# Reordered first stage, one-operation normalisation and DMA-turned last projections in an attention and feed-forward kernel

## The chip, the cores and the metric

One core of one Trainium2 chip runs the whole program. The metric is the device time of one execution in microseconds (us), lower is better. Durations of single operations come from one profiled execution.

## What is computed

A transformer block on x of 4 x 1024 x 512: layer norm without scale, causal attention with 16 heads of width 32, and a gated feed-forward of width 1536 whose weights are rounded to fp8 values. Both branches read the normalised x, and both are added to x.

```python
xn = _layernorm(x, axis=-1)
q, k, v = xn @ Wq.T, xn @ Wk.T, xn @ Wv.T            # split into 16 heads
scores = einsum('bhqd,bhkd->bhqk', q, k) / sqrt(32)  # causal mask, softmax
attn = einsum('bhqk,bhkd->bhqd', probs, v) @ Wo.T
fuse = silu(xn @ gate_w8 * gate_scale) * (xn @ up_w8 * up_scale)
out = x + attn + (fuse @ down_w8) * down_scale
```

## The kernel before

TensorE works on fp16. A float32 operand is split into a high and a low fp16 part (HI, LO), and a product is the sum of three terms, HI x HI, HI x LO and LO x HI (`TERMS`). Each engine has its own program, written out by hand; tables of step numbers (`PROJ_STEP`, `GATE_STEP`, `HEADS_LOADED` and so on) say at which step an engine does what, and semaphores couple the engines. Nothing is scheduled by a planner. SP issues nearly all DMAs, in the order of its program; a wait in it holds up every DMA behind it.

**First stage** (`prepare`). x is taken in 8 tiles of 512 tokens. A tile is 12 chunks of 12 matmuls of 512 columns: four chunks for q, four for k, four for v (L904). ACT copies each chunk's high part out of PSUM (L575, L579), DVE subtracts for the low part (L796, L800), SP stores it. Beside that, for the next tile: DVE takes the statistics (L601, L605) and normalises (L615), POOL computes the reciprocal root in 14 small operations (L468 to L476) and the low part of x (L485), ACT the high part (L512, `x_high`), and SP turns both parts by DMA transposes (L382, `turn_x`). TensorE begins a tile when both parts are turned. Only tile 0 is turned on TensorE, and so are the weights (L842, `turn_weights`), which need a power-of-two scale: DVE takes a maximum (L634, `weights_max`), TensorE spreads it over the partitions (L867, `spread_max`), DVE reads it back (L652, `weights_power`). DVE also rounds the feed-forward weights in 24 parts (`magnitude`, `add_step_of`, `take_step_off`). A chain of small DVE operations (L747 to L760, `feed_forward_factors`) follows the last chunk, and then all engines meet at the end of the block.

**The loop** (`attend`). 16 iterations of 4 heads, each head in 9 steps, 36 steps k to an iteration. In every head TensorE computes transposed scores (L1426), row scores (L1440, L1444) and the row maxima of a later head (L206), and multiplies probabilities with values (L1464). ACT does the exponentials, ACT, POOL and DVE the splitting, and SP turns the last two rows of probabilities (L1073). `normalise` on DVE (L1302 to L1316) closes each half of a head:

```python
nc.vector.tensor_copy(o_low[:, :, :], o_half[:, :, 0:DK])
nc.vector.reciprocal(rsum[:, :], o_half[:, :, 2 * DK])
nc.vector.tensor_tensor(o_sum[:, :, :], o_half[:, :, DK:2 * DK], o_low[:, :, :], ALU.add)
nc.vector.tensor_tensor(dst, o_sum, rsum broadcast, ALU.mult)
```

The feed-forward of two blocks of 128 tokens is spread over an iteration (L1488, L1502). From iteration 4 on, the output projection of two blocks is added (L1519): ACT and POOL split them into `a_part` (steps 12 and 20), SP turns them (L1110), TensorE projects at steps 20 to 22 and 28 to 30, DVE adds the result (L1331), SP stores it. Each head's maxima reach TensorE through a small DMA (L196, `store_row`), which the next head's first scores wait for.

**The end.** The last iteration leaves eight blocks to project. TensorE first finishes the last head's values and two feed-forward blocks (L1502). DVE scales these (L1340), POOL adds them (L1143), and then POOL makes the low parts (L1147). TensorE turns each block by 8 transposes (L1512), DVE copies it out of PSUM (L1323), TensorE projects. There are two buffers.

Of the kernel before, what the change touches and what calls it, by code (L numbers as in the profile page):

```python
# [37 lines left out]
TERMS = ((HI, HI), (HI, LO), (LO, HI))  # L38
EPS = 1e-5
# [23 lines left out]
FF_LOADED = {(1, 0): ((0, 1), (1, 1)),  # L63
             **{(t, 6): ((2, t),) for t in range(1, NT - 1)},
             **{(t, 8): ((0, t + 1),) for t in range(1, NT - 1)},
             **{(t + 1, 0): ((1, t + 1),) for t in range(1, NT - 1)}, (NT - 1, 4): ((2, NT - 1),)}
X_LOADED = {**{(t, 4): t + 2 for t in range(1, NT - 2)}, (0, 7): 2}


HEADS_LOADED = {(2, 3): 0, (2, 6): 1, (3, 3): 2}  # L70
# [69 lines left out]
GATE_STEP = {4: 0, 6: 1, 8: 2, 14: 3, 16: 4, 18: 5, 19: 6, 23: 7, 25: 8, 27: 9, 31: 10, 33: 11}  # L140
# [128 lines left out]
def prepare(nc, x, weights, ffn, scales, xn_dram, keep, rows, bank):  # L269
# [11 lines left out]
    with ExitStack() as ctx:  # L281
# [6 lines left out]
        w_raw = [sb(f"w_raw{m}", [P, KC, D], F32) for m in range(3)]  # L288
# [85 lines left out]
        def _(sp):  # L374
            def turn_x(w, t):
# [14 lines left out]
            for m in range(3):  # L390
                load_weights(m)
            sp.wait_ge(w_hi_done, 1)
# [3 lines left out]
            def tile(t, par):  # L396
# [11 lines left out]
                for c in range(8):  # L408
# [9 lines left out]
                    if (t, c) == (NT - 1, 3):  # L418
                        store_row(sp, rows, 0, 1)
                    dst = (q_dram if c < 4 else k_dram).rearrange(  # L420
# [74 lines left out]
        def wmax_bank(m):  # L495

            return bank[(2, 2, 5, 0)[m]][:, 0:P]
# [6 lines left out]
        def _(act):  # L504
# [38 lines left out]
            def load_scales():  # L543
                gate_s, up_s, down_s = scales
                with nc.allow_non_contiguous_dma(reason="two vectors of 1536 scales"):
                    act.dma_start(gs[:, :], gate_s.rearrange("(c p) -> p c", p=P)).then_inc(small_loaded, 16)
                    act.dma_start(us[:, :], up_s.rearrange("(c p) -> p c", p=P)).then_inc(small_loaded, 16)
                act.dma_start(ds_row[:, :], down_s.rearrange("(a d) -> a d", a=1).broadcast_to([P, D])).then_inc(
                    small_loaded, 16)

# [14 lines left out]
            def tile(t, par):  # L565
                for c in range(12):
# [18 lines left out]
                    if (t, c) == (5, 2):  # L585
                        load_scales()
# [8 lines left out]
        def _(dve):  # L595
# [92 lines left out]
            weights_power(1)  # L688

# [72 lines left out]
            def factors_of_weights():  # L762
# [7 lines left out]
            first_tile = {0: ("max 2",), 1: ("power 2",), 2: ("statistics",), 3: ("low 2",), 4: ("normalise",),  # L770
                          6: ("magnitude 0",), 7: ("add 0",), 8: ("off 0", "magnitude 1"), 9: ("add 1",), 11: ("off 1",)}
            last_tile = {0: ("magnitude 20", "add 20"), 1: ("off 20",), 2: ("magnitude 21",), 3: ("add 21",),
                         4: ("off 21", "magnitude 22"), 5: ("add 22",), 6: ("off 22",), 7: ("magnitude 23", "add 23"),
                         8: ("off 23",), 9: ("maxima",), 11: ("factors",)}

            def plan_of(t):
                if t in (0, NT - 1):
                    return last_tile if t else first_tile
                a, b, c = (f"{3 * t - 1 + i}" for i in range(3))
                w3 = {(2, 11): ("max 3",), (3, 5): ("power 3",), (4, 11): ("low 3",)}  # L780
                return {0: ("statistics",), 1: ("magnitude " + a,), 2: ("normalise",), 3: ("add " + a,),
                        4: ("off " + a, "magnitude " + b), 5: ("add " + b,) + w3.get((t, 5), ()), 6: ("off " + b,),
                        7: ("magnitude " + c,), 8: ("add " + c,), 9: ("off " + c,),
                        11: w3.get((t, 11), ())}

            def tile(t, par):
                plan = plan_of(t)
                for c in range(12):
                    for m in WEIGHTS_COPIED.get((t, c), ()):
                        copy_weights(m)  # L790
                    if t == c == 0:
                        weights_low(1)
                    dve.wait_ge(hi_done, 12 * t + c + 1)
# [8 lines left out]
                    for what in plan.get(c, ()):  # L802
# [19 lines left out]
                        elif has_next(t):  # L822
                            {"statistics": norm_statistics, "normalise": normalise}[name](t + 1)
# [11 lines left out]
        def _(pe):  # L835
# [32 lines left out]

            pe.wait_ge(ident_set, 1)
# [4 lines left out]
            spread_max(1)  # L874

            def tile(t, par):
                for c in range(12):
                    if c == 0:

                        if t == 0:  # L880
                            pe.wait_ge(xt_act, 2)
                            pe.wait_ge(xt_dve, 2)
                        else:
                            for w in range(2):
                                pe.wait_ge(x_turned[w], 16 * t)
                    if t == 0 and c in (0, 3):

                        pe.wait_ge(wpow_set, 2 + c // 3)
# [7 lines left out]
                    for wp, xp in TERMS:  # L896
                        for kc in range(KC):
# [3 lines left out]
                            else:  # L901
# [3 lines left out]
                                                  stop=((wp, xp) == TERMS[-1] and kc == KC - 1))  # L905
# [6 lines left out]
                    if t >= NT - 2:  # L912
# [6 lines left out]
                        if head == 1 and c == 0:  # L919
                            turn_maxima(nc, pe, rows, bank[7], ident, 0)  # L920

            over_tiles(tile)

            pe.wait_ge(rows.m_red, 2 * NM)
            pe.wait_ge(ffspread, 1)
            nc.tensor.matmul(bank[0][:, :], ones[:, :], spread[:, :, :].rearrange("p n q -> p (n q)"), start=True,
                             stop=True).then_inc(ffmax_mm, 1)
# [3 lines left out]
def attend(nc, x, out, xn_dram, keep, rows, pair, bank):  # L931
# [5 lines left out]
    with ExitStack() as ctx:  # L937
# [22 lines left out]
        o_low = sb("o_low", [P, QB // 2, DK], F32)  # L960
# [3 lines left out]
        xt = sb("xt", [P, 2, KC, FT], F16)  # L964
# [6 lines left out]
        o_sb = [sb(f"o_sb{i}", [P, D], F32) for i in range(2)]  # L971
# [5 lines left out]
        o_sum = o_bank[:, 512 - QB // 2 * DK:512].rearrange("p (i d) -> p i d", d=DK)  # L977

        q_loaded, v_loaded, row_loaded, mt_copied = rows.q_loaded, rows.v_loaded, rows.row_loaded, rows.mt_copied
        xt_loaded = sem("xt_loaded")  # L980
# [32 lines left out]
        turn_mm = sem("turn_mm")  # L1013
        turned = sem("turned")
        late_turned = sem("late_turned")
# [22 lines left out]
        def row_width(r):  # L1038
# [5 lines left out]
        late_part = [probs[0][:, HI, i * 2 * D:(i + 1) * 2 * D].rearrange("p (w d) -> p w d", w=2)  # L1044
                     for i in range(2)]
        late_t = [probs[0][:, LO, i * 2 * D:(i + 1) * 2 * D].rearrange("p (w k t) -> p w k t", w=2, k=KC)
                  for i in range(2)]

        def late(i, r):

            return 2 * (r - (NIT - LAG)) + i
# [6 lines left out]
        def _(sp):  # L1058
# [7 lines left out]
            load_tile(0)  # L1066
# [9 lines left out]
            def iteration(it, with_out):  # L1076
                for s in range(HEADS_PER_IT):
# [19 lines left out]
                    if with_out and s in (1, 2):  # L1097
                        turn_attention(s - 1, it - LAG)
# [19 lines left out]
            for r in range(NIT - LAG, NIT):  # L1118
                for i in range(2):
# [572 lines left out]
```

## Time and profile before

| | us |
|---|---|
| three runs, median (lowest to highest) | 1330.88 (1330.05 to 1332.48) |
| profiled execution, its own time | 1335.85 |
| its span, first to last instruction | 1334.1 |
| tile 0 of the first stage | 0 to 69.19 |
| tiles 1 to 5 | 69.19 to 236.04 |
| tiles 6 and 7 | 236.04 to 304.55 |
| between the stages | 304.55 to 309.33 |
| loop and the last head | 309.33 to 1285.98 |
| the end | 1285.98 to 1334.1 |

Busy shares of the span: TensorE 94%, DVE 81%, ACT 67%, POOL 65%. The share is a mean over stages with different limits. A row of the timeline gives start, duration, engine, line and operation, and in brackets how long the engine sat idle before it and who ended that. A run of matmuls on one line is merged (x24); its end is modelled and reaches a little past the start of the next one.

### The profile page before, as it was taken

Reading aid. Unit: us, or ns where it says so; the run is one execution under the profiler, and the core shown is the slowest. Engines: PE = TensorE matmul, PEld = TensorE weight load, DVE = VectorE, ACT = ScalarE, POOL = GpSimd, SP = SyncE. Lnnn points to the kernel's source line nnn. Section 1 sums busy time; section 2 is a strip of 40 time slices with the busy share of each in tenths; the row PEclk is TensorE's granted clock in tenths of the full one; section 3 lists DMA queues with packets and bytes.
Section 4 is the critical chain, followed back from the end, with each engine's and each line's share of the span. In section 5 each row is a group of like instructions: output and inputs, shape, how many; then the busy total and the mean of one; then the engine's idle time right before and its main releaser. Section 6 shows DMA issues by size and latency. Waiting matters only on the chain.

```text
span 1334.1 us, 32685 instructions
## 1 busy us (share of the span) xinstructions
PE 1253.1 (94%) x11812; PEld 829.4 (62%) x11813; DVE 1076.6 (81%) x2752; ACT 895.9 (67%) x1527; POOL 871.5 (65%) x1016
## 2 busy tenths in 40 slices
PE   4999999997898999999999999999999999999987
PEld 2444444344776667676767676677767676676754
DVE  7777778777888888888888798988888888888753
ACT  3322223225878787788878787888878787888841
POOL 1322222204777777787888788878878888888753
PEclk8999999997999999999999999999999999999999
DMA  7489899664555554567656675756675666756441
GB/s 255 116 240 255 238 237 231 180 169 111 110 121 126 118 128 93 129 116 164 120 138 138 119 159 122 160 108 148 121 155 120 139 141 126 157 120 155 81 91 64
DMA packets 419152, 193.98 MB, mean 145 GB/s; under 512 B 330800, under 2 KB 388144, under 8 KB 418992
## 3 DMA queue, kind: packets, MB, share of 16 engines
q1 hardware_dynamic: 397328, 174.84, 57.9%
q10 hardware_dynamic: 21664, 17.05, 4.6%
q8 instruction: 94, 1.54, 0.5%
q14 instruction: 66, 0.54, 0.1%
HBM read 72.89 MB, written 42.21 MB: 86 GB/s over the span
## 4 chain that ended last, share of the span: by engine, by line
PE 33%; POOL 16%; ACT 8%; DVE 7%; issue 6%; DMA 4%; SPq 2%; ACTq 0%; DVEq 0%
PE bank L1488 12%; POOL row L1169 8%; PE bank L1502 8%; PE bank L1464 5%; DMA xt<-xn_parts 3%; POOL fuse L1151 3%; PE pair L206 3%; PE pair L1426 3%; ACT probs L1216 2%; SPq L1073 2%; ACT row L1240 2%; ACT fuse L1255 2%; POOL probs L1035 2%; PE pair L1519 2%; DVE row_top L1359 2%
## 5 line engine op out<-in xcount | busy, mean ns | idle before, releaser
L1226 ACT ACTIVATE p<-pair,s_exp 128x512 f32<-128x512 f32 (+1 forms) x384 | 243.3, 634 | 161.2 <-PE pair L1426 159.7
L1169 POOL TENSOR_TENSOR row<-row 128x896 f16<-128x896 f32 (+1 forms) x128 | 256.1, 2010 | 11.5 <-ACT row L1240 11.4
L1216 ACT CAST probs<-p 128x512 f16<-128x512 f32 (+1 forms) x384 | 214.7, 559 | 14.4 <-POOL p L1163 13.5
L1035 POOL TENSOR_TENSOR probs<-p,probs 128x512 f16<-128x512 f32 x192 | 221.2, 1156 | 0.2
L1488 PE MATMUL bank<-xt,wg 128*128 128x256 f16 x1536 | 204.1, 277 | 7.2 <-DMA xt<-xn_parts 4.7
L1488 PE MATMUL bank<-xt,wu 128*128 128x256 f16 x1536 | 204.0, 277 | 0.0
L1502 PE MATMUL bank<-wd,fuse 128*128 128x512 f16 x768 | 190.6, 378 | 0.9 <-DVE ff_out L1340 0.9
L1163 POOL TENSOR_SCALAR_AFFINE_SELECT p<-p 128x128 f32<-128x128 f32 (+1 forms) x256 | 108.5, 428 | 110.6 <-ACT p L1226 108.6
L1359 DVE TENSOR_REDUCE row_top<-pair 128x1 f32<-128x896 f32 (+1 forms) x128 | 147.2, 1150 | 24.0 <-PE pair L1444 24.0
L1488 PEld LDWEIGHTS bank<-xt,wg 128*128 128x128 f16 x1536 | 141.8, 99 | 36.8 <-DMA xt<-xn_parts 11.0
L1488 PEld LDWEIGHTS bank<-xt,wu 128*128 128x128 f16 x1536 | 144.3, 99 | 23.0 <-issue 0.2
L1151 POOL TENSOR_TENSOR fuse<-fu,fuse 128x512 f16<-128x512 f32 x96 | 113.9, 1186 | 63.1 <-ACT fuse L1255 62.8
L1233 ACT ACTIVATE row<-pair,row_bias,s_exp 128x896 f32<-128x896 f32 (+1 forms) x128 | 148.2, 1158 | 0.5 <-DVE row_bias L1362 0.3
L1426 PE MATMUL pair<-q_st,k_st 98*128 98x256 f16 (+3 forms) x640 | 137.4, 280 | 6.3 <-PEq L281 4.8
L229 DVE CUSTOM_DVE_ANT_0 junk<-pair,mask 128x128 bf16<-128x128 f32 x252 | 117.0, 483 | 29.9 <-PE pair L206 27.5
L1464 PE MATMUL bank<-v_sb,probs 128*128 128x65 f16 x2688 | 134.0, 192 | 2.8 <-DVE attn L1314 2.8
L206 PE MATMUL pair<-k_st,q_st 96*128 96x128 f16 x504 | 125.4, 309 | 11.1 <-issue 6.4
L1464 PEld LDWEIGHTS bank<-v_sb,probs 128*128 128x128 f16 x2688 | 119.6, 97 | 25.8 <-issue 3.2
L1240 ACT CAST row<-row 128x896 f16<-128x896 f32 (+1 forms) x128 | 126.7, 990 | 0.0
L1035 DVE TENSOR_TENSOR probs<-p,probs 128x512 f16<-128x512 f32 (+1 forms) x192 | 124.6, 662 | 2.3 <-ACT probs L1216 2.3
L1347 DVE SCALAR_TENSOR_TENSOR ga<-th,bank 128x256 f32<-128x256 f32 x192 | 79.7, 415 | 34.3 <-ACT th L1247 32.8
L1502 PEld LDWEIGHTS bank<-wd,fuse 128*128 128x128 f16 x768 | 68.3, 97 | 60.2 <-DVE ff_out L1340 1.4
(153 smaller groups left out, 2160.0 us busy)
## 6 DMA issues: line engine op xcount, KB each, us to landing
q_st<-q_parts SPq DMA_DIRECT2D x192, 64.0 KB, 2.6
k_st<-k_parts SPq DMA_DIRECT2D x192, 64.0 KB, 2.0
v_parts<-res SPq DMA_DIRECT2D x8, 1056.0 KB, 6.5
v_sb<-v_parts SPq DMA_DIRECT2D x64, 132.0 KB, 2.2
xn_parts<-x_t SPq DMA_DIRECT2D x16, 512.0 KB, 7.6
q_parts<-qk_st SPq DMA_DIRECT2D x32, 256.0 KB, 4.5
k_parts<-qk_st SPq DMA_DIRECT2D x32, 256.0 KB, 4.1
xt<-xn_parts SPq DMA_DIRECT2D x16, 512.0 KB, 4.6
```

The costliest lines, as they stand in the source:

```text
L206: nc.tensor.matmul(banks[u % len(banks)][:, 0:w], rows.q_st[i][part, blk * P:(blk + 1) * P], rows.k_st[i][part, k0:k0 + w], start=True, st ...
L1035: ops.tensor_tensor(probs[n % 2][:, LO, at], p32[e % RING][:, 0:UNIT_WIDTH[u]], probs[n % 2][:, HI, at], ALU.subtract).then_inc(signal, 1)
L1151: nc.gpsimd.tensor_tensor(fuse_pair(LO, p), fu[p % FU][:, :], fuse_pair(HI, p), ALU.subtract).then_inc(fuse_lo, 1)
L1169: nc.gpsimd.tensor_tensor(row16[r][:, w:2 * w], row32[r][:, :], row16[r][:, 0:w], ALU.subtract).then_inc(row_lo, 1)
L1216: nc.scalar.copy(probs[n % 2][:, HI, u * 512:u * 512 + w], p32[e % RING][:, 0:w]).then_inc(p_hi, 1)
L1226: nc.scalar.activation(p32[e % RING][:, 0:w], st_bank[u % 2][:, 0:w], ACT.Exp, scale=s_exp[:, :]).then_inc(exp_done, 1)
L1240: nc.scalar.copy(row16[r][:, 0:row_width(r)], row32[r][:, :]).then_inc(row_hi, 1)
L1359: nc.vector.tensor_reduce(row_top[:, r:r + 1], row_bank[r][:, 0:row_width(r)], AX.X, ALU.max).then_inc(row_red, 1)
L1426: mm = nc.tensor.matmul(st_bank[u % 2][:, at:at + w], k_st[s][:, j * P:(j + 1) * P], q_st[s][:, q0:q0 + w], start=True, stop=True)
L1464: mm = nc.tensor.matmul(o_half[:, i % (QB // 2), :], probabilities(n, i, j, part), v_sb[s][:, j, 0:VN], start=(j == 0 and part == HI), sto ...
L1488: mm = nc.tensor.matmul(ff_bank[f % 2][:, h * FT:(h + 1) * FT], (wg8, wu8)[h][:, kc, f * P:(f + 1) * P], xt[:, part, kc, :], start=(part = ...
L1502: mm = nc.tensor.matmul(misc[:, :], fuse[:, part, f, i * P:(i + 1) * P], wd8[:, f, :], start=(f == 0 and part == HI), stop=(f == FC - 1 an ...
```

## The change

- `X_TERMS`: in the first stage the term with the low part of x comes last, and `x_half_there` lets TensorE begin a tile when the high part is turned; the low part is waited for before the third group of four matmuls of chunk 0.
- Tile 0: the spreading of the second weight's maximum moves behind chunk 0, the third weight's maximum (`weights_max(2)`) ahead of the tiles, the third weight is turned after chunk 5 (before: 4) and evacuated at chunk 6 (before: 5); the second is turned after chunk 2 as before, and DVE evacuates it a chunk earlier.
- Each later tile: x is split (`x_high`) after chunk 2 (before: 4), the turns stand behind the stores of chunks 3 and 5 (before: 5 and 7), statistics are taken at chunk 10 of the tile before, normalisation at chunk 0. Feed-forward parts are loaded and rounded about one part earlier; the three early heads are loaded at the start of tiles 3, 4 and 5. The scales are loaded by SP at the beginning, not by ACT in tile 5.
- End of the first stage: the spreading of the feed-forward maxima goes behind chunk 8 of tile 7, and the factors are computed at chunk 9. The first `xt` is loaded in tile 7. `w_raw[0]`, `xt` and `o_sb` share one buffer.
- Loop: `normalise` sums both halves in one reduction. Gate 6 moves from step 19 to 22, the first projection from 20..22 to 19..21, its addition from 23 to 22. SP issues the turn of `a_part` ahead of the output store and `store_row`. A small memset moves from DVE to POOL.
- The end: four buffers; SP turns the eight blocks; TensorE and DVE do no turning. POOL makes the first four low parts ahead of the two additions; the values of row block 3 are computed ahead of the feed-forward products.

```diff
+X_TERMS = ((HI, HI), (LO, HI), (HI, LO))
-WEIGHTS_SPLIT = {(0, 2): (2,), (3, 6): (3,)}
-WEIGHTS_COPIED = {(0, 3): (1,), (0, 5): (2,), (5, 8): (3,)}
-WMAX_SPREAD = {(0, 1): 2, (3, 3): 3}
-X_TURNED = {5: 0, 7: 1}
+WEIGHTS_SPLIT = {(0, 3): (2,), (3, 6): (3,)}
+WEIGHTS_COPIED_DVE = {(0, 2): (1,), (0, 6): (2,), (5, 8): (3,)}
+WEIGHTS_COPIED = {(0, 3): (1,), (0, 6): (2,), (5, 8): (3,)}
+WMAX_SPREAD = {(0, 0): 1, (0, 2): 2, (3, 3): 3}
+X_TURNED = {3: 0, 5: 1}
-HEADS_LOADED = {(2, 3): 0, (2, 6): 1, (3, 3): 2}
+HEADS_LOADED = {(3, 0): 0, (4, 0): 1, (5, 0): 2}
-PROJ_STEP = {20: [(0, 0)], 21: [(0, 1)], 22: [(0, 2)], 28: [(1, 0)], 29: [(1, 1)], 30: [(1, 2)]}
+PROJ_STEP = {19: [(0, 0)], 20: [(0, 1)], 21: [(0, 2)], 28: [(1, 0)], 29: [(1, 1)], 30: [(1, 2)]}
+NLATE = 4
-ADD_OUT_STEP = {23: 0, 31: 1}
+ADD_OUT_STEP = {22: 0, 31: 1}
...
-                    if c == (7 if t == 0 else 4) and has_next(t):
+                    if c == (7 if t == 0 else 2) and has_next(t):
                         x_high(t + 1)
...
-            spread_max(1)
...
+            def x_half_there(w, t):
+                if t == 0:
+                    pe.wait_ge(xt_act, w + 1)
+                    pe.wait_ge(xt_dve, w + 1)
+                else:
+                    pe.wait_ge(x_turned[w], 16 * t)
...
-                    for wp, xp in TERMS:
+                    for wp, xp in X_TERMS:
+                        if c == 0 and xp == LO:
+                            x_half_there(LO, t)
...
+                    if with_out and s in (1, 2):
+                        turn_attention(s - 1, it - LAG)
                     if with_out and s in (2, 3):
                         store_out(2 * (it - LAG) + s - 2, s - 2, it - LAG)
...
                     if n + 1 < NH:
                         store_row(sp, rows, (s + 1) % 4, n + 2)
-                    if with_out and s in (1, 2):
-                        turn_attention(s - 1, it - LAG)
...
+            def turn_late(b):
+                i, r = of_late(b)
+                sp.wait_ge(split_done, 2 * r + i + 1)
+                if b >= NLATE:
+                    sp.wait_ge(op_mm, 2 * (NIT - LAG) + b - NLATE + 1)
+                sp.dma_start_transpose(late_t[b % NLATE].rearrange("p w k t -> p (w k) t"),
+                                       late_part[b % NLATE].rearrange("p w d -> p (w d)")).then_inc(late_turned[b % NLATE], 16)
...
-            for i in range(2):
-                add_down(i, NIT - 1)
-            for r in range(NIT - LAG, NIT):
-                for i in range(2):
-                    low_of_attention(i, r, late_part[i], attention_rows(i, r))
+            for b in range(2 * LAG):
+                i, r = of_late(b)
+                low_of_attention(i, r, late_part[b % NLATE], attention_rows(i, r))
+                if b in (3, 5):
+                    add_down((b - 3) // 2, NIT - 1)
...
-                nc.vector.tensor_copy(o_low[:, :, :], o_half[:, :, 0:DK])
-                nc.vector.reciprocal(rsum[:, :], o_half[:, :, 2 * DK]).then_inc(o_link, 1)
...
+                nc.vector.reciprocal(rsum[:, :], o_half[:, :, 2 * DK])
+                nc.vector.tensor_reduce(o_sum[:, :, :], o_half[:, :, 0:2 * DK].rearrange("p i (w d) -> p i d w", w=2),
+                                        AX.X, ALU.add).then_inc(o_link, 1)
...
+            for b in range(2 * LAG):
+                i, r = of_late(b)
                 pe.wait_ge(o_ready, 2 * r + i - 1)
-                pe.wait_ge(late_turned, late(i, r) + 1)
+                pe.wait_ge(late_turned[b % NLATE], 16 * (b // NLATE + 1))
                 for piece in range(PROJ_PIECES):
-                    project(i, piece, r, bank[2 + i], late_t[i])
+                    project(i, piece, r, bank[2 + i], late_t[b % NLATE])
```

TensorE's order at the start, before (L867 spreads a maximum, L842 turns, L904 is the projection, 12 matmuls to a chunk):

```order
L842 MATMUL pair<-ident,x_part 128x128 x16
L842 MATMUL bank<-ident,x_part 128x128 x16
L867 MATMUL pair<-res 128x128
L904 MATMUL pair<-x_t,w_t 128x512 x24
L867 MATMUL bank<-res 128x128
L904 MATMUL bank<-x_t,w_t 128x512 x12
```

and now (the same three lines are L885, L860 and L933):

```order
L860 MATMUL pair<-ident,x_part 128x128 x16
L860 MATMUL bank<-ident,x_part 128x128 x16
L933 MATMUL pair<-x_t,w_t 128x512 x12
L885 MATMUL pair<-res 128x128
L933 MATMUL pair<-x_t,w_t 128x512 x12
L933 MATMUL bank<-x_t,w_t 128x512 x12
L885 MATMUL bank<-res 128x128
```

Chunk 0 now stands ahead of the second weight's maximum, and three chunks, not two, ahead of the third's.

SP's order in the second head of a full iteration, before (L196 stores the maxima, L1110 turns `a_part`, L1073 turns probabilities):

```order
L184 DMA k_st<-k_parts 32x1024 x3
L189 DMA v_sb<-v_parts 128x528
L196 DMA q_st<-m_row 2x6x128
L1110 DMA_TRANSPOSE a_t<-a_part 128x8x128
L1073 DMA_TRANSPOSE p_t<-row_0 128x14x128
```

and now (L199, L1133, L1096; the third head's output store is L1138):

```order
L192 DMA v_sb<-v_parts 128x528
L1133 DMA_TRANSPOSE a_t<-a_part 128x8x128
L1138 DMA out<-shared 128x512
L199 DMA q_st<-m_row 2x6x128
L1096 DMA_TRANSPOSE p_t<-row_0 128x14x128
```

This second list is the third head; in the second head the output store is missing and the rest is the same. The store of the maxima now stands behind the turn in both.

TensorE's end, before (L1512 turns, L1519 projects; five more such pairs follow):

```order
L1502 MATMUL bank<-wd,fuse 128x512 x28
L1512 MATMUL pair<-ident,probs 128x128 x16
L1519 MATMUL pair<-wo_t,probs 128x512 x12
L1512 MATMUL pair<-ident,probs 128x128 x8
L1519 MATMUL pair<-wo_t,probs 128x512 x12
```

and now (L1529 is L1502, L1537 is L1519; p_0 to p_3 are the four buffers):

```order
L1529 MATMUL bank<-wd,fuse 128x512 x28
L1537 MATMUL pair<-wo_t,p_0 128x512 x12
L1537 MATMUL pair<-wo_t,p_1 128x512 x12
L1537 MATMUL pair<-wo_t,p_2 128x512 x12
L1537 MATMUL pair<-wo_t,p_3 128x512 x12
```

All 64 transposes are gone from TensorE.

## Rows read from the trace of the kernel before

**Rows 1.** Windows: length, busy PE, PEld, DVE, ACT, POOL (instructions), clock, DMA share, GB/s.

```profile
69.19:236.04 166.85, 161.08 (x754) 72.80 (x755) 126.74 (x205) 48.27 (x68) 47.81 (x90) 0.98 0.91 238
...
383.99:567.89 183.90, 171.48 (x1885) 126.35 (x1884) 153.67 (x439) 148.14 (x258) 142.42 (x156) 0.97 0.54 118
567.89:1239.25 671.36, 661.00 (x7173) 476.39 (x7172) 577.05 (x1629) 553.74 (x968) 550.08 (x594) 1.00 0.64 136
```

**Rows 2.** Timeline of PE in the first stage.

```profile
25.78 0.29 PE L867 MATMUL pair<-res 128*128 128x128 bf16 x1 [3.64 <-DVE res L645]
26.61 7.81 PE L904 MATMUL pair<-x_t,w_t 128*128 128x512 f16 x24 [0.54 <-issue]
...
69.19 7.01 PE L904 MATMUL pair<-x_t,w_t 128*128 128x512 f16 x24 [2.20 <-issue]
...
136.31 7.03 PE L904 MATMUL pair<-x_t,w_t 128*128 128x512 f16 x24 [3.13 <-issue]
...
236.04 7.03 PE L904 MATMUL pair<-x_t,w_t 128*128 128x512 f16 x24 [2.23 <-issue]
...
299.21 5.34 PE L904 MATMUL bank<-w_t,x_t 128*128 128x512 f16 x24
```

**Rows 3.** Timeline of all engines in tile 0: ACT's high part of x.

```profile
57.18 1.90 ACT L512 CAST x_part<-xn 128x2048 f16<-128x2048 f32 x1
```

**Rows 4.** DMA issues: count, KB each, median us from issue to landing.

```profile
a_t<-a_part SPq DMA_TRANSPOSE x24, 3.4
...
x_t<-x_part SPq DMA_TRANSPOSE x14, 6.2
```

**Rows 5.** Timeline of all engines between the stages.

```profile
305.82 0.68 DVE L747 TENSOR_REDUCE ff4g<-pair 128x4 f32<-128x512 f32 x1
...
308.31 0.48 DVE L760 TENSOR_SCALAR ds_row<-ds_row,bound 128x512 f32<-128x512 f32 x1
...
309.33 1.01 PE L1426 MATMUL pair<-q_st,k_st 98*128 98x512 f16 x3 [4.78 <-PEq L281]
```

**Rows 6.** Timeline of DVE in iteration 1: first and last operation of `normalise`.

```profile
406.27 0.28 DVE L1306 COPY o_low<-bank 128x128 f32<-128x128 f32 x1
...
407.00 0.29 DVE L1314 TENSOR_TENSOR attn<-bank,rsum 128x128 f32<-128x128 f32 x1
```

**Rows 7.** Waits of PE from 565 to 1236: us in total, times, longest.

```profile
PE bank L1488 <- DMA xt<-xn_parts: 4.7, 8, 0.9
```

**Rows 8.** Timelines of POOL, SP and PE in one full iteration.

```profile
714.50 1.16 POOL L1147 TENSOR_TENSOR a_part<-attn,a_part 128x512 f16<-128x512 f32 x1
...
717.10 0.65 SPq L196 DMA_DIRECT2D q_st<-m_row  x1
717.86 1.26 SPq L1110 DMA_TRANSPOSE a_t<-a_part  x1
...
719.92 0.38 PE L1426 MATMUL pair<-q_st,k_st 98*128 98x512 f16 x1
...
731.53 0.65 SPq L196 DMA_DIRECT2D q_st<-m_row  x1
...
735.24 0.39 PE L1426 MATMUL pair<-q_st,k_st 98*128 98x512 f16 x1 [1.10 <-DMA q_st<-m_row]
```

**Rows 9.** Timeline of all engines at the end.

```profile
1292.21 1.10 PE L1464 MATMUL bank<-v_sb,p_t 128*128 128x65 f16 x30 [1.13 <-DVE attn L1314]
...
1295.71 5.35 PE L1502 MATMUL bank<-wd,fuse 128*128 128x512 f16 x24 [0.87 <-DVE ff_out L1340]
...
1306.24 3.74 PE L1519 MATMUL pair<-wo_t,probs 128*128 128x512 f16 x12
...
1310.26 2.75 PE L1519 MATMUL pair<-wo_t,probs 128*128 128x512 f16 x12
...
1313.30 2.75 PE L1519 MATMUL pair<-wo_t,probs 128*128 128x512 f16 x12
...
1330.83 0.75 DVE L1331 SCALAR_TENSOR_TENSOR o_sb<-pair,c_out,res 128x512 f32<-128x512 f32 x1 [1.84 <-PE pair L1519]
```

More of the change, by code:

```diff
@@ L286, in sem @@
             return ctx.enter_context(nc.semaphore(name))
-        w_raw = [sb(f"w_raw{m}", [P, KC, D], F32) for m in range(3)]
+        w_raw = [keep["shared"][:, :].rearrange("p (k d) -> p k d", k=KC)]
+        w_raw += [sb(f"w_raw{m}", [P, KC, D], F32) for m in (1, 2)]
         w_part = [sb(f"w_part{i}", [P, 2, KC, D], F16) for i in range(2)]
@@ L688, in _ @@
             weights_power(1)
+            weights_max(2)
             def raw_part(i):
@@ L767, in factors_of_weights @@
                 step(nc.vector.tensor_tensor(c_out[:, :], w_pow[:, 2:3], w_pow[:, 3:4], ALU.mult), 3)
[L770 to L774, printed above, removed]
+            first_tile = {3: ("statistics 1",), 4: ("low 2",), 5: ("normalise 1",),
+                          6: ("magnitude 0",), 7: ("add 0",), 8: ("off 0", "magnitude 1"), 9: ("add 1",),
+                          11: ("off 1", "statistics 2")}
@@ L776, in plan_of @@
             def plan_of(t):
-                if t in (0, NT - 1):
-                    return last_tile if t else first_tile
-                a, b, c = (f"{3 * t - 1 + i}" for i in range(3))
+                if t in (0, 1, NT - 1):
+                    return {0: first_tile, 1: second_tile, NT - 1: last_tile}[t]
+                a, b, c = (f"{3 * t + i}" for i in range(3))
                 w3 = {(2, 11): ("max 3",), (3, 5): ("power 3",), (4, 11): ("low 3",)}
-                return {0: ("statistics",), 1: ("magnitude " + a,), 2: ("normalise",), 3: ("add " + a,),
+                later = (f"statistics {t + 2}",) if t + 2 < NT else ()
@@ L782, in plan_of @@
+                return {0: (f"normalise {t + 1}",), 1: ("magnitude " + a,), 3: ("add " + a,),
                         4: ("off " + a, "magnitude " + b), 5: ("add " + b,) + w3.get((t, 5), ()), 6: ("off " + b,),
                         7: ("magnitude " + c,), 8: ("add " + c,), 9: ("off " + c,),
-                        11: w3.get((t, 11), ())}
+                        10: later, 11: w3.get((t, 11), ())}
             def tile(t, par):
@@ L878, in tile @@
                     if c == 0:
[L880 to L888, printed above, removed]
+                        x_half_there(HI, t)
+                    if t == 0 and c == 3:
+                        pe.wait_ge(wpow_set, 3)
                     if c % 4 == 0 and t == 0:
@@ L920, in tile @@
                             turn_maxima(nc, pe, rows, bank[7], ident, 0)
+                    if (t, c) == (NT - 1, 8):
+                        spread_ff_maxima()
             over_tiles(tile)
[L924 to L927, printed above, removed]
             pe.wait_ge(k_ones_set, 3)
@@ L970, in attend @@
         res = keep["res"]
-        o_sb = [sb(f"o_sb{i}", [P, D], F32) for i in range(2)]
+        o_sb = [keep["shared"][:, KC * FT + i * D:KC * FT + (i + 1) * D] for i in range(2)]
         st_bank, m_bank = bank[0:2], bank[2:4]
@@ L1040, in row_width, with of_late @@
             return (ROWS[r] + 1) * P
[L1044 to L1051, printed above, removed]
+        last_probs = probs[0][:, :, :].rearrange("p w e -> p (w e)")
+        late_part = [last_probs[:, b * 2 * D:(b + 1) * 2 * D].rearrange("p (w d) -> p w d", w=2) for b in range(NLATE)]
+        late_t = [p32[b][:, :].bitcast(F16).rearrange("p (w k t) -> p w k t", w=2, k=KC) for b in range(NLATE)]
+        def of_late(b):
+            return b % 2, NIT - LAG + b // 2
         def attention_rows(i, r):
@@ L1581, in _ @@
             start_values(NH - 1, 3, NIT, 3)
-            for i in range(3):
+            for i in range(4):
                 values(NH - 1, 3, i)
```

152 lines of the change are left out of this document (73 added, 79 removed).

## The prediction

> **What bounds it now.** I read the stages first, by windows, then TensorE's timeline in each, then who ends its waits. In tiles 1 to 5 TensorE is busy for 161.08 of 166.85 us while the DMA engines are busy for 0.91 of the time [rows 1]: the stage is TensorE's, with a transfer path close behind. The timeline shows where TensorE's time leaks. A tile begins after an idle stretch of 2.20, 3.13 or 2.23 us, and after each the first 24 matmuls take 7.01 to 7.03 us, against 5.34 for the same 24 at the end of the stage [rows 2]: these are the two levels of the clock, 1.2 GHz for part of the group and 2.4 GHz. So a gap costs its length and 1.7 us more. In full iterations (from 567.89 on) TensorE is busy for 661.00 of 671.36 us, so 0.94 us of each 61.0 is idle; in the three earlier ones 12.4 us of 183.90 is idle, 4.1 each, since they have no projection [rows 1]. At the end TensorE runs eight projections in turn with transposes, after a long pause. So the loop can give little, and the start and the end can give much.
>
> **Tile 0.** TensorE turned x by 22.14 (25.78 less the idle 3.64), then waited for the second weight's maximum, and began chunk 0 at 26.61 [rows 2]. Chunk 0 needs nothing of that maximum, and now stands ahead of it: 22.2, 4.4 us earlier. Its first 24 matmuls took 7.81 us, 2.5 over the fast 5.34; without the pause I take them as fast. If the clock is low all the same, 2.5 come back; I keep that for the range. The other waits of the tile I leave as they are: DVE's maximum of the third weight and the low part of that weight still come one after another. Tile 0 then ends at 66.99 - 4.4 - 2.5 = 60.1 (66.99 is 69.19 less 2.20).
>
> The next x follows the same seven chunks, so its high part ends at 59.08 - 6.9 = 52.2 [rows 3]. From there to the start of tile 1 were 10.1 us (POOL's low part and the second turn), which makes 62.3. TensorE can now run eight of chunk 0's twelve matmuls without the low part, 1.7 us of 2.6. It needs it at 61.8 and waits 0.5. Tile 1's effective start moves from 69.19 to 60.6: **8.6 us**.
>
> **Tiles 1 to 7.** x is split two chunks earlier, both turns are issued two chunks earlier (5.2 us), and the low part is needed 1.7 us later. That is 6.9 us of new slack against gaps of 3.13 and 2.23 us and a median landing of 6.2 us [rows 2, 4]. So both gaps go, 5.4 us, and the slow groups at 69.19, 136.31 and 236.04 with them, 1.67 + 1.69 + 1.69 = 5.0. Moving the three heads out of tile 2 and the scales out of tile 5 takes SP's issue time and many small packets from just the tiles whose successors began late; it is the same gain, not a second one. The scales wait on SP behind three weight loads, where SP would idle; I cost them at nothing, and if they did delay the fourth weight, that is not used before the end of tile 2. Earlier statistics and normalisation add nothing to DVE, busy for 126.74 of 166.85 us [rows 1]; where DVE must wait for POOL's root, TensorE has up to three chunks of finished PSUM ahead. Sum: **10.4 us**. Between none and all of it, I take all, by the slack.
>
> **Between the stages.** DVE's chain from 305.82 to 308.79 is what TensorE waits for until 309.33 [rows 5]. At chunk 9 it lies under three chunks (7.8 us) and may push the last low parts by some tenths. TensorE's pause of 4.78 shrinks to about 2.3: **2.5 us**, between 1.5 and 3. The clock will still fall at that place. The memset moved to POOL lies under the first scores on TensorE; if it delays the mask, some tenths come back.
>
> **Loop.** From the copy to the last multiplication of `normalise` are 0.73 us [rows 6]. The reduction reads 256 elements; one of 512 takes 0.68 [rows 5], so between 0.34 and 0.68, nearer the half. With the reciprocal ahead of it a half of a head saves about 0.18 us, between nothing and 0.3. Two of an iteration's eight lie on the path at a time. Full iterations have 0.94 us idle to give, and part of that is the wait for `xt`, 4.7 us in 8 places [rows 7], which follows POOL and SP and stays. The swap of gate 6 with the projection is neutral in full iterations (equal groups of matmuls), and lets the addition at step 22 be done when the maxima are turned at 24. I take 0.2 us for 12 iterations and 0.3 for 4: **3.6 us**; bounds are nothing, and all the idle time, 28 us, which needs every coupling to go at once.
>
> The turn of `a_part` now stands ahead of the store of the maxima on SP. In the third head the low part was ready at 715.66, the turn's issue takes 1.26, so with the output store the row's store starts near 717.4 instead of 717.10; it landed within 2.82 us, before TensorE's start at 719.92 [rows 8]. New landing 720.2 at the latest: up to 0.3 us of wait, which can eat the gain above. I count it inside the 3.6.
>
> **The end.** The values of block 3 now come ahead of the feed-forward products, so DVE normalises under them: the wait of 1.13 before 1292.21 goes, and the shorter `normalise` gives 0.2 more: 1.3. The second set of products ends at 1295.71 + 5.35 = 1301.06, the projections begin at 1306.24 [rows 9]. These 5.2 us (scaling, addition, low part, turn, copy in a row) go, since ACT, POOL and SP prepare four blocks under 44 feed-forward products: four POOL operations of 1.16 and four turns of 1.26, with a landing of 3.4 us [rows 4, 8]. The first projection at the slow clock costs 3.74 instead of 2.75: 1.0. The pitch of the later ones is 13.30 - 10.26 = 3.04 us, of which 2.6 are the products; seven times 0.44 is 3.1. SP must deliver one turn per 2.6 us and issues it in 1.26, one round ahead. Sum **10.6 us**; what is late next is the last addition and store, unchanged after TensorE's end. Here the row sets the price of eight transposes at 0.44 us. The Trainium skill ("TensorE: Matmul & The Clock Gate", Part 4: PE-mode transpose) gives about 275 ns for one in a kernel; by that 56 of them would be 15.4 us, and the forecast 12 us lower. The row decides.
>
> **Sum.** 8.6 + 10.4 + 2.5 + 3.6 + 10.6 = 35.7 us. The profiled execution took 1335.85, with a span of 1334.1, 5 us over the median of 1330.88; it becomes 1300, and the median **1295.2**.
>
> **Rivals.**
> - *The DMA engines fill up.* 0.91 of 166.85 is 151.8 us of DMA work; without gaps and slow groups tiles 1 to 5 last 158.1 us, so the share must rise to 0.96 [rows 1]. If it cannot rise above 0.91, the turns land late again and 8.7 us return: 1304. For it: the share. Against: stores may lag a whole tile, and only the turns have a date, now 6.9 us looser. 0.17.
> - *The row's store lands behind the turn.* Both are on SP's queue. If the row shares the engines with the turn until that has landed (715.66 + 3.4 = 719.06) and needs some time more, TensorE waits perhaps 0.8 us in the second and third head of 12 iterations: 24 x 0.8 = 19, 1314. For it: TensorE already waited 1.10 us for a row stored at 731.53 [rows 8]. 0.10. The Trainium skill ("DMA: Bandwidth & Descriptors", Two DMAs through the same engine are not ordered) says that descriptors of one queue start in order on an engine but are pipelined. By that the row starts behind the turn, which speaks against this move, but overlaps it; no row here shows the two in that order.
> - *Slower: the two run one after the other.* The row then starts at 719.06 and lands up to 2.82 later, 721.9, 2.0 us late at 24 places: 1295 + 47 = 1342. It decides from 35.7 / 24 = 1.5 us per place on. Against: other stores and loads overlap freely at 0.64 DMA share. 0.05.
> - *The reorder is eaten elsewhere*, no change: 0.02.
>
> **Numbers.** The forecast has 0.66. A measurement of this kernel tells 0.2% (2.7 us) from no change. Faster are the forecast and the first two rivals, 0.93; slower 0.05; same 0.02. The range takes the forecast with its open prices (down to 1286 with a richer loop and less wait between the stages, up with the low clock of tile 0 and a full SP queue) and the first rival: 1286 to 1310.
>
> **What would show it.** Right: tile 1 starts near 61 us with 24 matmuls in 5.3; no idle stretch over 1 us at a tile's start; TensorE enters the loop near 288; iterations of 60.8; eight projections at a pitch of 2.6 and no idle before them. Wrong: idle time released by a turn at a tile's start, a DMA share of 0.91 with the old length, or a wait for the maxima's store at the head starts of iterations 4 to 15.

## The result and the profile after

The change takes the median from 1331.18 to **1319.24 us** (four runs each; 1317.69 to 1321.17): a ratio of 0.9905, 95% interval 0.9883 to 0.9926. That is 12 us faster, clear of the interval but only a third of the 35.7 us that were added up; the forecast was 1295.2 and its range ended at 1310. The profiled execution took 1318.2 with a span of 1316.5.

I set the stages beside those of before, by TensorE's timeline. Its columns are start, duration, engine, line, operation, and in brackets the idle time before and its releaser. First stage of the changed kernel:

```profile
21.43 2.75 PE L933 MATMUL pair<-x_t,w_t 128*128 128x512 f16 x12
...
58.87 1.89 PE L933 MATMUL pair<-x_t,w_t 128*128 128x512 f16 x8
61.84 3.63 PE L933 MATMUL pair<-x_t,w_t 128*128 128x512 f16 x16 [1.08 <-DMA x_t<-x_part]
65.31 5.34 PE L933 MATMUL bank<-x_t,w_t 128*128 128x512 f16 x24
...
91.21 5.34 PE L933 MATMUL pair<-x_t,w_t 128*128 128x512 f16 x24
...
286.10 0.59 PE L1453 MATMUL pair<-q_st,k_st 98*128 98x512 f16 x3 [2.53 <-PEq L284]
```

This answers [rows 2, 5]. Chunk 0 starts at 21.43, not 26.61, and runs at the high clock (granted 1.00 over its 12 matmuls; before, 0.68 over the first 24). Tile 1 waits once, 1.08 us, for the low part of x, a little over the 1 us that the prediction allowed at a tile's start. From 65.31 on a tile follows a tile with no gap and no slow group, and the loop is entered at 286.10, not 309.33: 23.2 us earlier.

Windows of the changed kernel, for [rows 1] (same columns): tiles 1 to 5, then the same two stretches of the loop, three early iterations and eleven full ones.

```profile
58.87:217.37 158.50, 157.42 (x755) 72.19 (x753) 132.32 (x213) 48.09 (x68) 46.46 (x90) 1.00 0.98 255
...
362.87:549.67 186.80, 170.12 (x1886) 124.84 (x1884) 157.97 (x416) 148.35 (x258) 141.69 (x156) 0.98 0.55 116
549.67:1229.01 679.34, 664.91 (x7173) 476.24 (x7172) 573.95 (x1542) 555.64 (x968) 556.06 (x594) 1.00 0.63 134
```

The tiles take 158.50 us for 166.85, with the DMA share up from 0.91 to 0.98. But the loop has become **longer**: 186.80 for 183.90 and 679.34 for 671.36, with no matmul more. An early iteration takes 62.27 us (before 61.30), a full one 61.76 (61.03). From its entry to the last head's values the loop takes 1276.80 - 286.10 = 990.70 us, against 1285.98 - 309.33 = 976.65: 14.05 us are given back.

The end, TensorE's timeline of the changed kernel, for [rows 9]:

```profile
1276.80 0.77 PE L1491 MATMUL bank<-v_sb,probs 128*128 128x65 f16 x20 [2.85 <-DVE attn L1358]
1277.41 6.17 PE L1529 MATMUL bank<-wd,fuse 128*128 128x512 f16 x20
...
1286.83 5.35 PE L1529 MATMUL bank<-wd,fuse 128*128 128x512 f16 x24 [0.79 <-DVE ff_out L1376]
1292.02 20.88 PE L1537 MATMUL pair<-wo_t,p 128*128 128x512 f16 x96
```

Eight projections in 20.88 us, 2.61 each, with nothing between. The end takes 39.70 us, not 48.12.

**Where the loop lost it.** The new `normalise` on DVE, line L1358, by form (durations in ns: min/median/max), after:

```profile
L1353 DVE TENSOR_REDUCE o_sum<-bank x128: 385/394/397, 305.4 to 1285.3; 128x128 f32<-128x256 f32 x128
L1358 DVE TENSOR_TENSOR attn<-o_sum,rsum x128: 291/358/1276, 305.8 to 1285.7; 128x128 f32<-128x128 f32 x128
...
  PE bank L1491: 8.9, 27
```

and the same multiplication before:

```profile
L1314 DVE TENSOR_TENSOR attn<-bank,rsum x128: 290/291/292, 329.2 to 1294.8; 128x128 f32<-128x128 f32 x128
```

The reduction costs 0.39, as estimated. The multiplication behind it, the same operation on the same number of elements, was 0.29 every time; now it is up to 1.28, and TensorE waits for it 27 times, not 4. The name of its first operand has changed: `bank` is PSUM, `o_sum` is SBUF. One such place in the timeline of DVE and POOL, after:

```profile
441.35 0.18 DVE L1352 RECIPROCAL rsum<-bank 128x4 f32<-128x4 f32 x1
441.44 0.40 DVE L1353 TENSOR_REDUCE o_sum<-bank 128x128 f32<-128x256 f32 x1
...
441.81 1.16 POOL L1060 TENSOR_TENSOR probs<-p,probs 128x512 f16<-128x512 f32 x1
441.88 1.24 DVE L1358 TENSOR_TENSOR attn<-o_sum,rsum 128x128 f32<-128x128 f32 x1
...
443.04 0.41 DVE L1383 SCALAR_TENSOR_TENSOR ga<-th,bank 128x256 f32<-128x256 f32 x1
```

and the same half of a head before:

```profile
461.23 0.28 DVE L1306 COPY o_low<-bank 128x128 f32<-128x128 f32 x1
...
461.98 0.29 DVE L1314 TENSOR_TENSOR attn<-bank,rsum 128x128 f32<-128x128 f32 x1
462.26 0.42 DVE L1347 SCALAR_TENSOR_TENSOR ga<-th,bank 128x256 f32<-128x256 f32 x1
```

POOL begins at 441.81 and ends at 442.97; the multiplication begins at 441.88 and ends at 443.12, 0.15 later. So it is for all 67 multiplications over 0.35 us: each began under a POOL operation and ends 0.14 to 0.15 us behind that operation's end (for 15 of them it is the first of two that the timeline merges into one row of 2.32). Together they are 39.4 us longer than at 0.29. The other 61 fit too: 35 had no POOL operation beside them and in 13 POOL began later, all at 0.29; 13 began under a POOL operation with less than 0.2 us left and took 0.29 to 0.34. DVE's next operation comes 1.69 us after the first of `normalise`; before it came after 1.03. On average a half takes 1.12 us, not 1.03: where 0.18 was to be saved, 0.09 is lost, and up to 0.8 at the worst places.

TensorE's waits in the early iterations (total us, times, longest), before (363.99 to 567.89):

```profile
PE pair L1440 <- ACT p L1226: 5.7, 6, 1.3
PE pair L206 <- issue: 3.9, 6, 0.6
PE pair L206 <- DVE mx L229: 2.4, 3, 0.8
```

and after (342.71 to 549.51):

```profile
PE pair L1467 <- ACT p L1269: 6.3, 6, 1.1
PE pair L209 <- DVE mx L232: 5.4, 4, 1.4
PE pair L209 <- issue: 3.9, 6, 0.6
PE bank L1515 <- DMA shared<-xn_parts: 0.9, 2, 0.7
PE bank L1491 <- DVE attn L1358: 0.6, 3, 0.2
```

What is behind the multiplication on DVE comes late: the maxima `mx`, whose banks TensorE needs, up to 1.4 us. In full iterations (549 to 1229) the waits are these, beside [rows 7]:

```profile
PE pair L1453 <- DMA q_st<-m_row: 6.4, 8, 1.5
PE bank L1491 <- DVE attn L1358: 3.7, 20, 0.2
PE bank L1515 <- DMA shared<-xn_parts: 2.6, 4, 1.3
```

The second wait is for the multiplication itself. The first, 1.6 us before, is what the prediction's second rival spoke of. So two theories were open: **P**, the second operand in SBUF, and **R**, the turn of `a_part` ahead of the store of the maxima.

### The profile page after: what moved, and what is told of

Its sections match the earlier page's. It is cut to its first block, busy times and chain, and to the rows that moved or that the text cites. A ratio compares the mean times of both kernels' runs of the same rounds, so it can differ in the third digit from the quotient of the medians.

```text
span 1316.5 us, 32425 instructions
## 1 busy us (share of the span) xinstructions
PE 1240.5 (94%) x11749; PEld 819.5 (62%) x11749; DVE 1074.4 (82%) x2615; ACT 897.8 (68%) x1527; POOL 876.9 (67%) x1017
## 4 chain that ended last, share of the span: by engine, by line
PE 45%; DVE 14%; issue 5%; DMA 5%; ACT 4%; POOL 3%; SPq 2%; ACTq 0%; DVEq 0%; POOLq 0%
PE bank L1515 14%; PE bank L1529 10%; PE bank L1491 7%; PE pair L1453 4%; PE pair L209 4%; DVE probs L1060 3%; DMA shared<-xn_parts 3%; PE bank L1537 2%; DVE row_top L1395 2%; DMA q_st<-m_row 2%; PE pair L1467 2%; DVE junk L232 2%; ACT probs L1259 2%; POOL row L1212 2%; DVE ga L1383 2%
## 5 line engine op out<-in xcount | busy, mean ns | idle before, releaser
L1060 POOL TENSOR_TENSOR probs<-p,probs 128x512 f16<-128x512 f32 x192 | 223.0, 1165 | 0.2
L1515 PE MATMUL bank<-shared,wg 128*128 128x256 f16 x1536 | 201.9, 275 | 3.5 <-DMA shared<-xn_parts 3.5
L1515 PE MATMUL bank<-shared,wu 128*128 128x256 f16 x1536 | 202.4, 275 | 0.0
L1529 PE MATMUL bank<-wd,fuse 128*128 128x512 f16 x768 | 192.3, 381 | 0.8 <-DVE ff_out L1376 0.8
L1206 POOL TENSOR_SCALAR_AFFINE_SELECT p<-p 128x128 f32<-128x128 f32 (+1 forms) x256 | 104.0, 411 | 118.2 <-ACT p L1269 117.6
L1194 POOL TENSOR_TENSOR fuse<-fu,fuse 128x512 f16<-128x512 f32 x96 | 120.7, 1257 | 62.5 <-ACT fuse L1298 62.3
L1515 PEld LDWEIGHTS bank<-shared,wg 128*128 128x128 f16 x1536 | 142.5, 98 | 29.7 <-DMA shared<-xn_parts 8.0
L1515 PEld LDWEIGHTS bank<-shared,wu 128*128 128x128 f16 x1536 | 143.6, 99 | 22.1 <-issue 0.2
L1453 PE MATMUL pair<-q_st,k_st 98*128 98x256 f16 (+3 forms) x640 | 136.8, 279 | 10.4 <-DMA q_st<-m_row 7.4
L1060 DVE TENSOR_TENSOR probs<-p,probs 128x512 f16<-128x512 f32 (+1 forms) x192 | 113.7, 605 | 2.4 <-ACT probs L1259 2.4
L237 DVE TENSOR_REDUCE mx<-pair 128x1 f32<-128x512 f32 x128 | 87.8, 687 | 23.9 <-PE pair L209 23.9
```

What stands on the lines that cost most here:

```text
L1060: ops.tensor_tensor(probs[n % 2][:, LO, at], p32[e % RING][:, 0:UNIT_WIDTH[u]], probs[n % 2][:, HI, at], ALU.subtract).then_inc(signal, 1)
L1453: mm = nc.tensor.matmul(st_bank[u % 2][:, at:at + w], k_st[s][:, j * P:(j + 1) * P], q_st[s][:, q0:q0 + w], start=True, stop=True)
L1515: mm = nc.tensor.matmul(ff_bank[f % 2][:, h * FT:(h + 1) * FT], (wg8, wu8)[h][:, kc, f * P:(f + 1) * P], xt[:, part, kc, :], start=(part = ...
L1529: mm = nc.tensor.matmul(misc[:, :], fuse[:, part, f, i * P:(i + 1) * P], wd8[:, f, :], start=(f == 0 and part == HI), stop=(f == FC - 1 an ...
```

## The experiments

**1. The sum back in PSUM.**

```diff
-        o_sum = sb("o_sum", [P, QB // 2, DK], F32)
+        o_sum = o_bank[:, 512 - QB // 2 * DK:512].rearrange("p (i d) -> p i d", d=DK)
```

> The changed kernel, with one difference: the sum that normalise keeps between its reduction and its multiplication lies in PSUM again (the end of the bank of the values, where the kernel before had it), not in SBUF. Theory P (the multiplication now reads two operands from SBUF, and each time POOL is in one of its two-operand operations it lasts until that ends, 0.36 to 1.24 us and not 0.29): all 128 multiplications take 0.29, a half of a head takes 0.81 and not 1.12 on average, the early iterations fall from 62.3 us to 61.3 or below, the full ones from 61.8 to 61.0, and the time from 1319 to 1302 to 1305. Theory R (the store of the maxima lands late, since the turn of a_part is now ahead of it on SP's queue): only iterations 4 to 15 have that turn, they stay near 61.6, and the time falls to 1313 to 1316 at most.

Measured: 1303.3 us (ratio 0.9778, interval 0.9741 to 0.9815), full iterations 60.89. By form:

```profile
L1358 DVE TENSOR_TENSOR attn<-bank,rsum x128: 290/291/292, 304.6 to 1270.9; 128x128 f32<-128x128 f32 x128
```

16 us come back from one line, with the reduction kept. The early iterations took 61.98, less of a fall than P said; in the other runs without stretched multiplications they took 60.7 to 62.1, so single executions scatter there.

**2. The turn back behind the store**, in SP's order, the sum left in SBUF.

```diff
-                    if with_out and s in (1, 2):
-                        turn_attention(s - 1, it - LAG)
...
                         store_row(sp, rows, (s + 1) % 4, n + 2)
+                    if with_out and s in (1, 2):
+                        turn_attention(s - 1, it - LAG)
```

> The changed kernel with SP's old order: the turn of a_part behind the store of the maxima. Theory P: TensorE's waits for the stored maxima (6.4 us in iterations 4 to 14) may go, but the multiplications stay long, the early iterations stay at 62.3 and the time at 1316 to 1320. Theory R: iterations 4 to 15 fall from 61.8 to 61.0, 9 us in all, and the time to 1310; the early iterations, which have no such turn, stay.

Measured: 1317.81 (0.9885, 0.9847 to 0.9923), 1.4 us under the changed kernel; early iterations 62.18, full ones 61.86. These are P's numbers, and R, which said 1310, falls as the main cause.

**3. Both.**

> Both edits in one: sum in PSUM, and the turn behind the store. Theory P: as the first, 1302 to 1305, within 2 us of it. Theory R: as the second less what the sum alone gives, 1304 to 1308, 9 us below the first.

Measured: **1298.24** (0.9747, 0.9703 to 0.979), the best of all and 21 us under the changed kernel. It is 5.1 us below the first experiment, which neither theory had (P within 2, R 9): beside P the turn does seem to cost something.

**4. The other way round:** the kernel before, with its sum in SBUF.

```diff
-        o_sum = o_bank[:, 512 - QB // 2 * DK:512].rearrange("p (i d) -> p i d", d=DK)
+        o_sum = sb("o_sum", [P, QB // 2, DK], F32)
```

> The kernel before, with one difference: its sum lies in SBUF and not in PSUM; SP's order, the steps and the first stage are the old ones. Theory P: the multiplications stretch under POOL as in the changed kernel, on top of the older and longer three operations ahead of them; iterations grow by 1.0 to 2.0 us and the time from 1331 to 1345 to 1363. Theory R: nothing of the queue is touched, 1329 to 1333.

Measured: 1378.11 (1.0332, 1.0284 to 1.0379), 46 us slower, above P's 1363.

```profile
L1314 DVE TENSOR_TENSOR attn<-o_sum,rsum 128x128 f32<-128x128 f32 x128 | 90.9, 710 | 4.4
L1309 DVE TENSOR_TENSOR o_sum<-bank,o_low 128x128 f32<-128x128 f32 x128 | 37.3, 291 | 4.4
```

The multiplication takes 710 ns on average, a half of a head 1.44 us, 0.41 more: 128 x 0.41 = 52 us, of which 46 show in the time. Here 85 of the 128 take over 0.35 us, and each of them again ends 0.14 to 0.15 us behind a POOL operation. The addition L1309, with one operand in PSUM and one in SBUF, stays at 291.

**5. The sum in SBUF, but the reciprocals in PSUM.**

```diff
-        rsum = sb("rsum", [P, QB // 2], F32)
+        rsum = o_bank[:, 512 - QB // 2:512]
```

> The changed kernel, with the sum left in SBUF and the four reciprocals of a half put into PSUM instead. Theory P as it stands after the first runs (what counts is that the multiplication has two operands in SBUF): now it has one, so all 128 last 0.29 to 0.30 us under POOL and the time is that of the sum in PSUM, 1301 to 1306. Rival Q (it is the place of the sum: a reduction's result in SBUF is slow to read back): the multiplications stay at 0.6 on average and the time at 1316 to 1321.

Measured: 1302.21 (0.9785, 0.976 to 0.9811).

```profile
L1358 DVE TENSOR_TENSOR attn<-o_sum,bank x128: 286/286/289, 305.9 to 1269.8; 128x128 f32<-128x128 f32 x128
```

The sum lies in SBUF as in the change, and nothing waits. So it is the number of SBUF operands that counts, not the place of the sum. No run takes POOL's operations away; that POOL is the other party is read from the ends of the long multiplications and from the short ones that had no POOL operation under way.

**6. The whole `normalise` of before** (copy, reciprocal, addition, multiplication) in the changed kernel.

> The changed kernel with the whole normalise of the kernel before: copy, reciprocal, addition into PSUM, multiplication, 1.03 us for a half and not 0.81 as with the reduction into PSUM (measured 1303.3). It prices the reduction where nothing stretches. As the prediction counted it (0.2 us an iteration on the path): 1306 to 1308. If DVE's normalise is off the path in full iterations: 1302 to 1304. If each half is on the path: 0.22 x 8 x 16 = 28 us, 1331.

Measured: 1306.38 (0.9814, 0.9789 to 0.9839). The reduction, where nothing stretches, is worth 3.1 us beside the first experiment, and 4.5 and 4.1 in the two other pairs of the table below: about the size of the prediction's term. Each lies within its runs' intervals.

**7 and 8. The old steps**, with the turn behind (7) and ahead (8), the sum in PSUM in both.

```diff
-GATE_STEP = {4: 0, 6: 1, 8: 2, 14: 3, 16: 4, 18: 5, 22: 6,
+GATE_STEP = {4: 0, 6: 1, 8: 2, 14: 3, 16: 4, 18: 5, 19: 6,
-PROJ_STEP = {19: [(0, 0)], 20: [(0, 1)], 21: [(0, 2)],
+PROJ_STEP = {20: [(0, 0)], 21: [(0, 1)], 22: [(0, 2)],
-ADD_OUT_STEP = {22: 0, 31: 1}
+ADD_OUT_STEP = {23: 0, 31: 1}
```

> Sum in PSUM and turn behind the store (measured 1298.2), and in addition the old steps: gate 6 at step 19, the first projection at 20 to 22, its addition at 23. If the steps are neutral, as the prediction has it: 1296 to 1300. If the earlier projection is what the maxima's transpose needs (the addition done when they are turned at 24): 1300 to 1306.

> As the last, but with the turn ahead of the store of the maxima, as the change has it; beside the last it prices the turn's place alone, with the old steps, beside the 5.1 us between the two runs with the new steps (1303.3 and 1298.2). If the turn ahead of the store delays that store (theory R): 4 to 9 us above the last, 1301 to 1308. If it does not, and the 5.1 us were a chance: within 2 us of the last.

Measured: 1300.34 (0.9784, 0.976 to 0.9808) and 1303.88 (0.9802, 0.9781 to 0.9824). The first lies just above the neutral range, too near it to decide. The second is 3.5 us above the first, between the two expectations.

**9 and 10. The loop of before** in the changed kernel (9), and the same with the new steps (10).

> The changed kernel with all three edits of the loop undone: the normalise of the kernel before, the turn behind the store of the maxima, the old steps. What is left of the change is the first stage, the place between the stages and the end. By the prediction's terms for these (8.6 + 10.4 + 2.5 + 10.6 = 32.1) under 1331: 1299. By the stages of the changed kernel's trace (loop entered 23.2 us earlier, end 8.4 us shorter): 1299 to 1300. If the earlier loads and the shared buffer have slowed the loop by themselves: 1303 or more, with iterations over 61.3.

> The changed kernel with the normalise of the kernel before and the turn behind the store; the new steps stay. Beside the run with the old normalise alone (1306.4) it prices the turn's place a fourth time: if the turn ahead costs what the three pairs so far gave (1.4, 5.1, 3.5), 1301 to 1305, with 2 to 3 us less of TensorE's waits for the stored maxima; if that was a chance, 1305 to 1308. Beside the run with all of the loop undone it prices the steps alone: neutral within 2 us.

Measured: 1304.45 (0.9801, 0.9784 to 0.9817), full iterations 61.19; and 1302.78 (0.9785, 0.9767 to 0.9803). The ninth misses the expected 1299 to 1300. Its time is that of the third case, a slowed loop, but its iterations are not over 61.3; the next section says where the difference lies. The tenth has the expected time, but its waits for stored maxima in full iterations did not fall (6.6 us, against 6.1 in the sixth). All medians together:

| us | sum in SBUF | sum in PSUM | old `normalise` |
|---|---|---|---|
| new steps, turn ahead | 1319.24 | 1303.30 | 1306.38 |
| new steps, turn behind | 1317.81 | 1298.24 | 1302.78 |
| old steps, turn ahead | | 1303.88 | |
| old steps, turn behind | | 1300.34 | 1304.45 |

Down a column, the turn ahead costs 1.4, 5.1, 3.6 and 3.5 us; the new steps gain 0.6, 2.1 and 1.7. Each of these differences lies within its runs' intervals, and the kernel before had medians of 1330.28 to 1332.45 in the sets that are compared here, so only their common sign speaks for them. Along a row, the sum in SBUF costs 15.9 and 19.6, far outside.

## Why the prediction was right and wrong

**Tile 0** (8.6): right against the trace that it was read from. Tile 1's group ends at 65.31; with two chunks of 2.59 taken off, it began in effect at 60.13 (predicted 60.6), 9.1 earlier. The low part was waited for 1.1 us, not 0.5.

**Tiles 1 to 7 and between the stages** (10.4 + 2.5): right against the same trace; *The offset* below says what that hides. From 60.13 to the loop's entry are 225.97 us, before 240.14: 14.2. The pause is 2.53 (predicted 2.3). The prediction had the clock fall at its end. It did not: the first scores take 0.59 us and not 1.01 [rows 5]. It fell some 2 us later, behind two more waits of 0.67 and 1.19 us (granted 0.96 from 286.1 to 288.5, then 0.50 to 294), and from the loop's entry to the second group of gate products 9.8 us pass in both kernels.

**The end** (10.6): 8.4. The order, the pitch and the missing pause are as predicted: the pause gives 5.3 us. What is lacking is mainly the start, where 1.3 was to be gained and 0.3 was lost: behind a wait of 2.85 us, not 2.42, the clock fell (granted 0.72 from 1277.41 to 1283.42, 1.00 before), and 20 feed-forward products took 6.17 us, not 4.48. The sum also counted seven sets of transposes between the projections; before, the last two projections followed each other without one, so six times 0.44 was there to gain.

**The loop** (3.6): here it failed. The step is "with the reciprocal ahead of it a half of a head saves about 0.18 us, between nothing and 0.3". It priced the operation that was added (the reduction, correctly) and those removed, and took the multiplication behind them as it was: "nothing" was no lower bound. The declaration of `o_sum` had moved from PSUM to SBUF, which neither the list of the change nor the prediction mentions. The loop lost 14.05 us in the trace where 3.6 were to be gained: 17.65 of the 18.2 us by which the profiled execution missed its 1300. Experiment 1 moves that line back and gets 15.9 us, to 1303.3, inside the range; experiment 4 adds it to the old kernel and loses 46.

The trace of before did show it, at another line: DVE's subtraction for the low parts, whose two operands lie in SBUF.

```profile
L1035 DVE TENSOR_TENSOR probs<-p,probs x192: 279/684/2040, 312.5 to 1285.8; 128x512 f16<-128x512 f32 x128, 128x128 f16<-128x128 f32 x64
```

The row mixes two shapes. Of the 128 operations of the larger one, 43 take over 0.75 us and up to 2.04, where the shortest take 0.68; each of the 43 ends 0.54 to 0.55 us behind the end of a POOL operation. The multiplication and the addition, which read PSUM, have no spread at all. A line with a spread beside lines without is a question to ask before an operand is moved. The Trainium skill ("SBUF — State Buffer", Who interferes with whom) has the rule: a DVE instruction with two SBUF inputs contends with a GpSimd instruction that reads SBUF, and the ports that they share go to whoever issues first, for the whole instruction, while the other blocks fully. By that the 67 long multiplications end where POOL's operations end, which the trace shows, and experiments 1 and 5, with one SBUF input, do not wait, which they show too. The changed kernel's trace also has the other order: POOL's operations L1060 that began 0.08 us after a multiplication took 1.23 us and not 1.16, and operations that began 0.18 us after one were not longer. There POOL waited for 0.07 us, less than the 0.21 us that the multiplication still had to run.

**The offset.** The sum was made against the profiled execution, and the 4.97 us by which that lay above the median were carried over to the result. They did not carry: the changed kernel's profiled execution lay 1.0 below its median. That is the other 6 us of the miss. Where the 4.97 us lay, experiment 4 shows, whose first stage is that of the kernel before:

```profile
67.22 5.34 PE L904 MATMUL pair<-x_t,w_t 128*128 128x512 f16 x24 [2.21 <-issue]
...
230.84 5.34 PE L904 MATMUL pair<-x_t,w_t 128*128 128x512 f16 x24
...
302.44 1.01 PE L1426 MATMUL pair<-q_st,k_st 98*128 98x512 f16 x3 [4.56 <-PEq L281]
```

Beside [rows 2, 5], tile 1 has its gap but no slow group, tile 6 has neither gap nor slow group, and the loop is entered at 302.44, not 309.33. So the same first stage took 6.9 us less in this execution, and the terms of the first stage counted the removal of gaps and slow groups that not every execution has: from 302.44 to 286.10 are 16.3 us, not 23.2. With that entry, the loop and the end of the trace before give a span of 1327.2 (an estimate), near the median. Experiment 9 fits: its span is 31.4 us under the trace before, where the terms for its parts say 32.1, but its median only 26.1 under the median. How often the first stage runs either way is not shown.

**The rivals.** The DMA engines did not fill up: the share rose to 0.98, above the 0.96 that was needed. *The row's store behind the turn* gave 1314, near the measured time, and was not the main cause: turned back alone, the order is worth 1.4 us of the 19 that the rival counted, some 3 us over four pairs. The mechanism is there, at few places. The rows stored behind a turn are those for the third and fourth head. With the turn ahead TensorE waits there for 1.4, 2.7, 2.0, 2.6 and 2.8 us in all (the changed kernel, experiments 1, 5, 6, 8), at three to five places and not at 24; with the turn behind it never waits there (experiments 2, 3, 7, 9, 10). One such place, in experiment 1 and then in experiment 3:

```profile
637.62 0.39 PE L1453 MATMUL pair<-q_st,k_st 98*128 98x512 f16 x1 [1.11 <-DMA q_st<-m_row]
```

```profile
635.34 0.38 PE L1453 MATMUL pair<-q_st,k_st 98*128 98x512 f16 x1
```

The other seven of ten waits for a stored row in the changed kernel stand at the first head of an iteration, where no turn is ahead of the store, and such waits come with either order. What brings them, and whether the first kind is all of the 3 us, stays open. Slower and unchanged did not come; faster at 0.93 held.

## What to carry to other kernels

When an edit moves a small buffer from PSUM to SBUF, look at every DVE operation that reads it: if its other operand is in SBUF too, expect it to last, as here, until the POOL operation under which it began has ended. Price the operations behind an edit too, not only those it replaces; an unchanged operation with a new operand is a changed one. And do the sum against an execution that took the median time, or do not count what only a slower execution has.

## What was not expected of the hardware

A DVE multiplication of 128x128 elements took 0.29 us with one operand in PSUM, whichever of the two that was, and 0.29 to 1.28 with both in SBUF, always ending 0.14 to 0.15 us after an operation of POOL if it was stretched. The whole effect was 16 to 20 us on the changed kernel, and 46 on the one before. And 24 matmuls that were 7.0 us at a tile's start [rows 2] took 5.34 at the starts of tiles 2 to 5 without the gap, while the DMA engines were busy for 0.98 of the time in tiles 1 to 5.
